# Four-layer gated block on one core: norms moved to the end of expert layers, and the second attention's bias added by VectorE

## What is computed

```python
x = x + tanh(g_xattn[n]) * attention_n(layernorm(x), ctx)
x = x + tanh(g_ffn[n])   * experts_n(layernorm(x))          # n = 0, 1, 2, 3
# attention 1 (the "second attention"), 16 heads of 8 features:
scores = q k^T / sqrt(8) + adj;  scores = where(mask == 0, -inf, scores)
out = softmax(scores) v @ Wo.T + bo
# experts 0: 8 selu experts of width 512, the best two of each token weighted, with a gate network
# experts 1: the "bit layer": two linear layers whose inputs are rms-normed and rounded to 8 bit,
#            whose weights are rounded to -1, 0, 1, with a gelu between them
# experts 2: 8 silu experts of width 256 with low-rank additions, best two of each token
# attention 3: one wide head ("class attention"); experts 3: 16 small experts for each of 8 slices ("head experts")
```

## Time and profile before

| | before |
|---|---|
| median of three runs | 1921.5 us |
| the profiled execution | 1916.38 us, its span 1914.6 us |
| TensorE busy | 1348.0 us (70%), mean granted clock 0.841 of full speed |
| VectorE busy | 987.2 us (52%) |
| ScalarE busy | 751.5 us (39%) |
| POOL busy | 402.5 us (21%) |

### The profile page before, as it was taken

How to read it: one execution, slowest core, us unless ns; L and a number is a source line. 1 busy time by engine, 2 the same in 40 slices (tenths; PEclk the granted TensorE clock), 3 DMA queues, 4 the chain that set the end, 5 groups by cost and what they waited for, 6 DMA issues and landing times.

```text
span 1914.6 us, 21114 instructions
## 1 busy us (share of the span) xinstructions
PE 1348.0 (70%) x7836; PEld 666.6 (35%) x7836; DVE 987.2 (52%) x2268; ACT 751.5 (39%) x1102; POOL 402.5 (21%) x462
## 2 busy tenths in 40 slices
PE   3456978865647697867477797886473869886756
PEld 2223544441212334531222455444121233453211
DVE  3347546656563453462552664666656445346252
ACT  0034643522324143337266463353232413433636
POOL 4306020025030200015332601001503020001424
PEclk9988999987559898969578898999755989896969
...
DMA packets 49221, 78.57 MB, mean 41 GB/s; under 512 B 15056, under 2 KB 34272, under 8 KB 48496
## 3 DMA queue, kind: packets, MB, share of 16 engines
...
## 4 chain that ended last, share of the span: by engine, by line
PE 53%; DVE 18%; issue 12%; ACT 9%; DMA 4%; POOL 3%; SPq 1%; POOLq 0%; ACTq 0%; DVEq 0%
PE ps L705 5%; PE ps L587 5%; PE ps L721 5%; PE ps L538 5%; DVE nm L1205 4%; PE ps L809 4%; PE ps L863 3%; PE ps L543 3%; PE ps L811 3%; PE ps L852 3%; PE ps L799 3%; ACT hT L1075 3%; DVE ps L1221 2%; PE ps L570 2%; DVE hT L1403 1%
## 5 line engine op out<-in xcount | busy, mean ns | idle before, releaser
L341 POOL TENSOR_TENSOR rstd<-vare,mhalf 128x4 f32<-128x4 f32 x40 | 42.4, 1063 | 1191.2 <-DVE vare L1145 1131.2
L1205 DVE TENSOR_REDUCE nm<-ps 128x4 f32<-128x1024 f32 x192 | 231.8, 1222 | 113.9 <-PE ps L543 113.1
L965 ACT ACTIVATE pT<-ps 128x1024 f32<-128x1024 f32 x192 | 194.2, 1026 | 166.9 <-DVE ps L1221 103.8
L1075 ACT ACTIVATE hT<-ps,w_l_b 128x512 f32<-128x512 f32 x256 | 158.2, 684 | 91.6 <-PE ps L852 89.8
L705 PEld LDWEIGHTS ps<-l_ring,hT 128*128 128x128 f32 x1152 | 154.1, 206 | 79.7 <-issue 78.0
L705 PE MATMUL ps<-l_ring,hT 128*128 128x128 f32 x1152 | 157.8, 291 | 26.6 <-DVE acc L1343 25.1
L1403 DVE SCALAR_TENSOR_TENSOR hT<-ex,rl 128x512 f32<-128x512 f32 x144 | 104.4, 730 | 123.2 <-ACT rl L1014 99.2
L721 PE MATMUL ps<-xT,l_ring 128*128 128x512 f32 x288 | 164.9, 664 | 4.0 <-ACT rl L1014 4.0
L1013 ACT ACTIVATE ex<-ps,l_exp_bias 128x512 f32<-128x512 f32 x144 | 99.2, 689 | 172.3 <-PE ps L721 171.8
L852 PE MATMUL ps<-ex,w1s 96*128 96x512 bf16 x256 | 101.5, 438 | 75.2 <-ACT hT L1075 49.8
L587 PE MATMUL ps<-pT,vA 128*32 128x256 f32 x1536 | 122.8, 447 | 33.0 <-ACT oT L945 31.3
(11 more groups left out here) (256 smaller groups left out, 2097.7 us busy)
## 6 DMA issues: line engine op xcount, KB each, us to landing
...
```

What stands on the lines that cost most here:

```text
L965: act.activation(pT[:, v % NPB, :], scores, ACT.Exp).then_inc(sem("p_ready"), 1)
L1075: act.activation(hid3[:, n % 8, :], bank(5 + n % 2), ACT.Gelu, bias=W["l3_b1"][:, ep:ep + 1])\
L1205: dve.tensor_reduce(nm[:, 2 * b:2 * b + 2, :, j].rearrange("p t g -> p g t"), ps[:, sl:sl + 2, :].rearrange("p g (t k) -> p g t k", t=2), ...
```

## The change

Six things are done together.

1. The norm for the next attention of a turn moves from the start of that attention to the end of the turn's expert layer (`next_norm`, `next_T`, at position `OVER[n]`), and the experts of the next step wait on PE for it (`start_experts`). Attentions 1, 2 and 3 begin with k, q and v at once.
2. Of the twelve copies of `qS` six stay on SyncE and six go to POOL's queue (`queries`), behind the twelve copies of `kS`.
3. In the second attention the bias matmuls of the max slots, 64 an attention, and `query_bias` are gone. The bias of the query side stays in f32 (`bq`), and VectorE runs four `tensor_tensor_reduce` in a max slot, each on 128 x 256 elements: it adds `bq` in place in PSUM and takes the maximum. One negation a batch follows. A `tensor_tensor_reduce` is two instructions, the second of which writes the maximum out.
4. The bit layer starts later in its step and is spread: first quantising at positions 6 to 14, second at 28 to 38.4, end at 54.
5. The bias for the odd turn of S3 and S11 is made at the end of S2 and S10.
6. `FIRST_SLOT` goes from 25 to 18, so that fewer expert slots stand ahead of an attention's first max slot.

```diff
-FIRST_SLOT, SLOT = 25.0, 1.3
+FIRST_SLOT, SLOT = 18.0, 1.3
...
             def bias(i, side):
 
+                to = (bq, bfull)[side]
                 pool.wait_ge(sem("masks_loaded"), 16 * (2 * i + side + 1))
-                step(pool.tensor_scalar(bfull[:], m1[:], 0.0, NEG, ALU.is_equal, ALU.mult))
+                if i and not side:
+                    pool.wait_ge(*upto("max_ready", place(i - 1, 1), 2 * NK))
+                step(pool.tensor_scalar(to[:], m1[:], 0.0, NEG, ALU.is_equal, ALU.mult))
                 for b in range(NB):
-                    step(pool.tensor_tensor(bfull[:, 2 * b:2 * b + 2, :], bfull[:, 2 * b:2 * b + 2, :],
+                    step(pool.tensor_tensor(to[:, 2 * b:2 * b + 2, :], to[:, 2 * b:2 * b + 2, :],
                                             (W["adj_q"], W["adj_k"])[side][:], ALU.add))
-                if side:
-                    pool.engine_nop().then_inc(sem("bfull_ready"), 1)
-
-            def query_bias(i):
-
-                step(pool.tensor_copy(b1q[:, 0], bfull[:]))
-                step(pool.tensor_tensor(bfull[:], bfull[:], b1q[:, 0], ALU.subtract))
-                step(pool.tensor_copy(b1q[:, 1], bfull[:]))
-                pool.engine_nop().then_inc(sem("b1q_ready"), 1)
+                pool.engine_nop().then_inc(sem(("bq_ready", "bfull_ready")[side]), 1)
 
             def keys(m):
 
@@ -379,36 +375,40 @@
                         pool.dma_start(kS[row:row + DH, :, :], kp[64 * g:64 * g + 64, part, :])\
                             .then_inc(sem("k_stack"), 16)
 
+            def queries(m):
+
+                pool.wait_ge(*upto("qp", m, 1))
+                for n, part in enumerate(X_PARTS):
+                    row = 64 + DH * n
+                    pool.dma_start(qS[row:row + DH, :, :], qp[64:128, part, :]).then_inc(sem("q_stack_1"), 16)
+
             def attention(i, a):
 
                 yield 1.0
-                if a == 3:
-                    root(i)
-                else:
+                if a < 3:
                     attention_over(pool, (i, a))
-                    root(i)
+                    if a == 0:
+                        root(i)
                     yield 3.0
                     keys(place(i, a))
+                    yield 5.0 if a else 11.0
+                    queries(place(i, a))
                     if i % 2 and a == 0:
-                        yield 10.0
...
+                        yield 20.0
                         mask_in(i + 1, 0)
+                        yield END - 12.0
+                        bias(i + 1, 0)
+                        mask_in(i + 1, 1)
                     if a == 1 and i % 2:
-                        yield 5.0
-                        bias(i, 0)
-                        mask_in(i, 1)
-                        yield 12.0
-                        query_bias(i)
-                        yield 22.0
+                        yield 16.0
...
             def experts(i, n):
 
-                yield 0.0
                 if n == 1:
-                    root(i)
-                    yield 16.0
+                    for at in BIT_ROOTS:
+                        yield at
+                        root(i)
+                if n < 3:
+                    yield OVER[n] + 1.0
                     root(i)
...
@@ -518,21 +520,21 @@
                 yield 0.0
                 start_attention(i, a)
                 pe.matmul(bank(0), W[L + "wk"][:], cT[s][:], start=True, stop=True).then_inc(sem("k_ps"), 1)
+                if a == 0:
+                    yield 6.0
+                    norm_T(i, LN_OF_ATT[a])
+                    yield 7.5
+                pe.wait_ge(*of("xT_ready", i, 7, n_T(LN_OF_ATT[a])))
+                pe.matmul(bank(3), W[L + "wq"][:], xT[s][:], start=True, stop=True).then_inc(sem("q_ps"), 1)
                 for t in range(NT):
                     last = pe.matmul(bank(1)[:, t * P:(t + 1) * P], cT[s][:, t * P:(t + 1) * P], W[L + "wv"][:],
                                      start=True, stop=True)
                 last.then_inc(sem("v_ps"), 1)
-                yield 6.0
-                norm_T(i, LN_OF_ATT[a])
-                yield 7.5
-                pe.wait_ge(*of("xT_ready", i, 7, n_T(LN_OF_ATT[a])))
-                pe.matmul(bank(3), W[L + "wq"][:], xT[s][:], start=True, stop=True).then_inc(sem("q_ps"), 1)
...
                 def scores_for_max(sl, n):
 
                     b, j = divmod(n, NK)
-                    bias = {0: [], 1: [b1q[:, 0, 2 * b:2 * b + 2, :], b1q[:, 1, 2 * b:2 * b + 2, :]],
-                            2: [l2_bias_q[:]]}[a]
+                    bias = [l2_bias_q[:]] if a == 2 else []
...
 
                 slots, times = slots_of(grouped(i, a))
                 yield times[0]
-                for name in ("k_stack", "q_stack"):
-                    pe.wait_ge(sem(name), 16 * HP * NSEG * (m + 1))
+                pe.wait_ge(sem("k_stack"), 16 * HP * NSEG * (m + 1))
+                for g in range(HP):
+                    pe.wait_ge(sem(f"q_stack_{g}"), 16 * NSEG * (m + 1))
                 pe.wait_ge(*upto("vf", m, 1))
...
+            def start_experts(i, n):
+
+                experts_over(pe, (i, n))
+                last = before((i, n), 1)
+                if last is not None and last[1] < 3:
+                    pe.wait_ge(*of("xT_ready", last[0], 7, n_T(LN_OF_ATT[last[1] + 1])))
+
+            def next_T(i, n):
+
+                norm_T(i, LN_OF_ATT[n + 1], 6)
+
...
                 s, m, L = i % 2, place(i, a), f"l{a}_"
-                src = x[s] if a else xn[s]
                 yield 0.0
                 if a == 0:
                     dve.wait_ge(sem(f"x_loaded_{s}"), 16 * (i // 2 + 1))
-                statistics(i, src)
-                yield 4.0
+                    statistics(i, xn[s])
+                    yield 4.0
+                    dve.wait_ge(sem(f"x_copied_{s}"), i // 2 + 1)
+                    normal(i, xn[s])
+                    yield 10.0
+                else:
+                    yield 3.0
+                dve.wait_ge(*upto("qf", m, 1))
+                step(dve.tensor_copy(qp[:, 0, :], qf[:]))
+                step(dve.tensor_tensor(rest_a, qf[:], qp[:, 0, :], ALU.subtract))
+                step(dve.tensor_copy(qp[:, 1, :], rest_a))
+                dve.tensor_tensor(qp[:, 2, :], rest_a, qp[:, 1, :], ALU.subtract).then_inc(sem("qp"), 1)
+                yield 10.5 if a == 0 else 5.0
                 dve.wait_ge(*upto("v_ps", m, 1))
                 heads = bank(1).rearrange("p (t h d) -> p t h d", t=NT, h=H)
...
                 def maxima(sl, n):
 
                     b, j = divmod(n, NK)
+                    if a == 1 and n == 0:
+                        dve.wait_ge(sem("bq_ready"), i + 1)
                     dve.wait_ge(*upto("s1", m, n + 1))
-                    dve.tensor_reduce(nm[:, 2 * b:2 * b + 2, :, j].rearrange("p t g -> p g t"),
-                                      ps[:, sl:sl + 2, :].rearrange("p g (t k) -> p g t k", t=2),
-                                      AX.X, ALU.max, negate=True).then_inc(sem("max_ready"), 1)
+                    if a == 1:
+                        for g in range(HP):
+                            for t in range(2):
+                                part = bank(sl + g)[:, t * S:(t + 1) * S]
+                                ins = dve.tensor_tensor_reduce(part, part, bq[:, 2 * b + t, :], 1.0, LOWEST,
+                                                               ALU.add, ALU.max, nm[:, 2 * b + t, g, j:j + 1])
+                    else:
+                        ins = dve.tensor_reduce(nm[:, 2 * b:2 * b + 2, :, j].rearrange("p t g -> p g t"),
+                                                ps[:, sl:sl + 2, :].rearrange("p g (t k) -> p g t k", t=2),
+                                                AX.X, ALU.max, negate=True)
+                    ins.then_inc(sem("max_ready"), 1)
                     if j == NK - 1:
                         dve.wait_ge(*upto("max_ready", m, n + 1))
                         row, parts = nm[:, 2 * b:2 * b + 2, :, :], nmp[:, 2 * b:2 * b + 2]
+                        if a == 1:
+                            step(dve.tensor_scalar(row, row, -1.0, None, ALU.mult))
                         step(dve.tensor_scalar(parts[:, :, :, 0, :], row, CAP, None, ALU.min))
...
+            def next_norm(i, n):
+
+                statistics(i, x[i % 2])
+                yield OVER[n] + 2.0
+                normal(i, x[i % 2])
...
                 for n, part in enumerate(X_PARTS):
-                    for g in range(HP):
-                        row = 64 * g + DH * n
-                        sp.dma_start(qS[row:row + DH, :, :], qp[64 * g:64 * g + 64, part, :])\
-                          .then_inc(sem("q_stack"), 16)
+                    row = DH * n
+                    sp.dma_start(qS[row:row + DH, :, :], qp[0:64, part, :]).then_inc(sem("q_stack_0"), 16)
...
 SLOT_0, SLOT_2 = 2.2, 4.2
+BIT_ROOTS = (7.0, 29.0)
+OVER = (SLOT_0 * (N0 + 8), 54.0, SLOT_2 * (N2 + 3) + 10.0)
```

115 lines of the change are left out of this document (56 added, 59 removed).

## The result

The changed kernel took 1980.5 us (median of four runs, 1971.7 to 1984.1) against 1926.5 before (with a fourth run of 1931.6 beside the three named above): a ratio of 1.027, 95% interval 1.021 to 1.032. It is slower by 2 to 3%, where I had said 1900 us and a range of 1868 to 1942. Its profiled execution has a span of 1969.8 us against 1914.6.

What follows compares the result with a forecast made beforehand. TensorE was taken to bound S2's max slots, VectorE to have little to spare beside the bit layer, and a chain of small pieces to hold up step starts; the terms summed to -18, 1898 against 1916.4, said as 1900, range 1868 to 1942.

Steps and rivals of the forecast that it cites:

- S2 and S10: Steps with max slots bound by TensorE: shorter max slots and earlier scores against a longer tail, -3 us each.
- The scores stand at about 26 to 28.: Start of S2 and S10: first scores at 26 to 28 us instead of 32.3, -4.3 us.
- Some 6 us of TensorE come later and lengthen the tail: +6.: End of S2 and S10: 3.2 expert slots left out earlier run where the expert layer is alone, +6 us.
- -4.8 in the max slots.: Max slots of S2 and S10: VectorE becomes the bound at 96% busy, 45.4 instead of 50.2 us.
- the starts are not shortened: Rival on POOL's shared queue: six steps give back some 4 us each, +24, about 1922 us; chance 0.18.
- The price of a slot: VectorE's max slot: four pairs of 0.43 us cost 1.75 us against 1.14 before, 9.8 us more an attention.
- the hidden read: Rival on VectorE's max slots: accumulator read wholly hidden, 1.36 us a slot, total 1875 us; chance 0.2.
- S3 and S11: Steps with the bit layer: first maximum 8.8 us earlier, max slots 14.5 us longer, net +6 us each.
- A wait for `qS` before the first scores of S3: Sign at S3's start: if it stood there instead of the bit layer's root, the whole account would be wrong.
- S4 and S12: First maximum at 26 instead of 37.7 us, -11.8; VectorE's max stretch +6.9; net -5 us each.
- S7 and S15: Steps where the norm stands bare, as in S6 and S14 but with less in front: +1.5 us each.
- The clock: TensorE's granted clock in S2's max slots: lowered by less work, to 0.87 at 28.9 us, it costs little.

Runs made afterwards that it cites:

- fillers: Four matmuls without use per max slot of the second attention put back on TensorE in the changed kernel: 2002.4 us, ratio 1.039 to the kernel before.
- 18.4: FIRST_SLOT at 18.4 instead of 18 in the changed kernel: 1958.5 us, ratio 1.016 to the kernel before.

## Why the prediction was wrong, step by step

- **S2 and S10 (forecast -3 each, measured +24.4 and +21.4).** This step failed, in three terms: the path to the first scores, the max slots, and the exp slots, which stood at nothing without a reason.
  - *"The scores stand at about 26 to 28."* They stood at 39.0. My chain put k's copy-out at 6.4 us, right behind the norm's; on ScalarE it stands behind an expert's activation and came at 12.1. And I let the last copy land 4.5 us after its issue; it took 11.4. In S2 it is 19.4 to 22.0 us with the split and 22.3 to 25.8 without, from the first issue of k to the first matmul of the max slots, where that waits for the copies. The earlier trace rows had it: 437.17 to 453.42 for twelve copies is 1.35 us each, about twice the 0.66 of an issue there.
  - *"Some 6 us of TensorE come later and lengthen the tail: +6."* The tail grew by 6.4, in every kernel with 18, so this term was right. But I also counted the earlier start as a gain, and it didn't exist.
  - *"-4.8 in the max slots."* They were 1.9 shorter, with VectorE at 87% where I had 96%. The exp slots, which I had left unchanged, are where the time went: what follows the last max slot grew by 19.7, of which 6.4 is the tail. Moving the constant by 0.4 gives back 11.6 of these 19.7 us (72.3 for 83.9), so most of the rest is the interleaving. I never compared the two orders beyond the first slot.
- **The rival "the starts are not shortened"** named the copies: 18 issues on POOL's queue, and its last copy of q lands last. That is what S2 shows: POOL's last copy of q landed 38.8 us into the step and the scores began at 39.0. But it priced this at 4 us a step, where S2's first scores came 11 to 13 later than forecast, the late k among them, and it said nothing of the exp slots. In S3, S4, S5 and S8 the starts did shorten, by 4 to 9 us.
- **The price of a slot** was forecast at 1.75 us and measured at 1.49 to 1.53, between the hidden read (1.36) and the forecast. The rule of the Trainium skill, VectorE: DVE Perf Modes, section "The DRAIN you can't avoid", that the next operation does not start until the pipeline has emptied, would have given 2.46; the trace does not agree with it, since the next addition starts 0.38 us after one that is 0.47 long. That section's last sentence on the gap, "A next op that is not held starts earlier", is the one that the trace bears out here; I had left it aside. The term that I worked on most was near its mark and decided little.
- **S3 and S11 (+6 each, measured +3).** Start: first maximum at 32.3 us instead of the forecast 29.2, with the copies of q ahead of the scores and not the bit layer's root. Max slots: VectorE full, as said, 38.8 us from first to last maximum instead of 47. A wait for `qS` before the first scores of S3 was one of the signs that I had named for the whole account being wrong.
- **S4 and S12 (-5 each, measured -1.3).** First maximum at 28.6 instead of 26; max slots 31.7 instead of 32.8 us. What follows the last maximum is 2.8 us longer than before; why was not traced.
- **S5 and S13** (-7, measured -3.9 and -6.7), **S6 and S14** (+2.5, measured +5.1 and +2.1) and S8 (-4, measured -4.7) came out in kind; S0 (-4) gained 1.2. **S7 and S15** (+1.5, measured +5) did not, and it isn't the norm: with the norm back at the start they are as long.
- **The clock** I set aside as costing little. It fell to 0.74, more than I allowed. That it costs little isn't shown: with fillers it came back to 0.94 and the time went up, but by the fillers' own work, and at 18.4, where it came back to 0.87, 7.3 us of TensorE's busy time in S2 went with it. That fewer bias matmuls alone don't lose is shown, by the bias on VectorE in the kernel before.
